# DeBERTa attention on one core: the keys' distance tables read back by 16 rows per transfer

## The reference

```python
rel = make_log_bucket_position(arange(S)[:, None] - arange(S)[None, :])
c2p_att = einsum('bhqd,hpd->bhqp', q, pos_k)      # the queries' table
c2p = take_along_axis(c2p_att, clip(rel + 64, 0, 127), -1)
p2c_att = einsum('bhkd,hpd->bhkp', k, pos_k)      # the keys' table
p2c = take_along_axis(p2c_att, clip(-rel + 64, 0, 127), -1).swapaxes(-1, -2)
probs = softmax((q @ k.T + c2p + p2c) / scale)
```

## Time and profile before

| | us |
|---|---|
| median of 3 runs | 2465.15 |
| lowest, highest | 2462.11, 2466.71 |
| the profiled execution | 2483.14 |
| its span | 2481.5 |
| PE busy | 1868.5 (75%) |
| DVE busy | 1613.3 (65%) |
| POOL busy | 1130.0 (46%) |
| ACT busy | 999.9 (40%) |

### The profile page before, as it was taken

The page is one execution under the profiler, slowest core; times in us unless marked ns, Lnnn a source line. Parts: engine busy times, 40 slices in busy tenths (PEclk is TensorE's granted clock), DMA queues, the critical chain, the costliest instruction groups (busy, mean ns, idle before and its releaser), DMA issues. The chain is left out here.

```text
span 2481.5 us, 47249 instructions
## 1 busy us (share of the span) xinstructions
PE 1868.5 (75%) x13556; PEld 1379.0 (56%) x13557; DVE 1613.3 (65%) x3925; ACT 999.9 (40%) x2052; POOL 1130.0 (46%) x1472
## 2 busy tenths in 40 slices
PE   5868887888888888888599997756243389999652
PEld 3436666766666676666366764433233168876321
DVE  8947777777768777777755551687765944443354
ACT  2436665656656666655123232432031033332000
POOL 4135555555555555553131210377640045554666
PEclk9979999999999999999799998877575589999876
DMA  4679999999999999999312200000010545547333
GB/s 156 212 251 334 324 335 331 317 324 309 343 313 339 323 337 328 336 329 287 108 50 68 68 0 3 0 0 1 0 51 17 203 124 154 155 146 125 104 107 114
DMA packets 296148, 460.84 MB, mean 186 GB/s; under 512 B 38316, under 2 KB 229532, under 8 KB 295964
## 3 DMA queue, kind: packets, MB, share of 16 engines
q1 hardware_dynamic: 267484, 392.06, 49.2%
q0 software_dynamic: 28480, 66.39, 10.4%
HBM read 236.91 MB, written 221.38 MB: 185 GB/s over the span
## 5 line engine op out<-in xcount | busy, mean ns | idle before, releaser
L986 DVE CUSTOM_DVE_ANT_0 c2p<-bank,c2p 128x512 f32<-128x512 f32 x512 | 351.2, 686 | 176.3 <-PE bank L882 161.8
L944 ACT ACTIVATE c2p<-c2p,neg_max 128x512 f32<-128x512 f32 x512 | 372.0, 727 | 14.9 <-DVE neg_max L986 14.9
L995 DVE COPY probsT<-bank 128x512 f32<-128x512 f32 x512 | 351.1, 686 | 5.2 <-PE bank L892 5.1
L959 ACT COPY a_stage<-bank 128x320 f32<-128x320 f32 (+1 forms) x512 | 211.4, 413 | 308.8 <-PE bank L851 234.5
L892 PE MATMUL bank<-ident,c2p 128*128 128x128 f32 x2048 | 316.4, 277 | 1.2 <-ACT c2p L944 0.9
L892 PEld LDWEIGHTS bank<-ident,c2p 128*128 128x128 f32 x2048 | 256.8, 144 | 10.2 <-issue 2.6
L2260 POOL DMA_INDIRECT p_x_tile<-y_d,p_token x160 | 152.9, 956 | 230.2 <-POOLq L1961 107.5
L863 PE MATMUL bank<-tab,k 96*128 96x320 bf16 (+1 forms) x512 | 159.0, 311 | 121.8 <-DVE b_stage L938 104.1
L882 PE MATMUL bank<-ident,p2c 128*128 128x128 f32 x1280 | 233.7, 282 | 0.0
L938 DVE COPY b_stage<-bank 128x288 f32<-128x288 f32 (+1 forms) x256 | 119.7, 468 | 103.3 <-issue 50.2
L877 PE MATMUL bank<-k,q 96*128 96x384 bf16 (+1 forms) x512 | 158.9, 310 | 31.7 <-issue 26.4
(11 more groups left out here) (295 smaller groups left out, 3959.9 us busy)
## 6 DMA issues: line engine op xcount, KB each, us to landing
p2c_d<-b_stage SPq DMA_DIRECT2D x64, 640.0 KB, 8.2
c2p_d<-a_stage SPq DMA_DIRECT2D x64, 640.0 KB, 5.8
p2c_d<-b_stage SPq DMA_DIRECT2D x64, 576.0 KB, 7.6
c2p_d<-a_stage SPq DMA_DIRECT2D x64, 576.0 KB, 6.0
p2c<-p2c_d SPq DMA_DIRECT2D x256, 144.0 KB, 4.6
c2p<-c2p_d SPq DMA_DIRECT2D x256, 144.0 KB, 5.1
o_sorted_d<-p_o_pair SPq DMA_DIRECT2D x80, 256.0 KB
p_w_all<-in_experts SPq DMA_DIRECT2D x4, 3072.0 KB, 21.9
```

The costliest lines, as they stand in the source:

```text
L944: act.activation(c2p[:, w % 4, j, :], c2p[:, w % 4, j, :], ACT.Exp, bias=neg_max[:, w % 2, j:j + 1], scale=-1.0).then_inc(exp_done, 1)
L959: act.copy(staged(a_stage, wa % 2, wa % TPB)[:, j, :], bank[A_BANK][:, 0:width(wa % TPB)]).then_inc(a_copied, 1)
L986: dve.tensor_tensor_reduce(c2p[:, w % 4, j, :], bank[S_BANKS[(HB * w + j) % 3]][:], c2p[:, w % 4, j, :], -SCALE, LOWEST, ALU.add, ALU.min, ...
L995: dve.tensor_copy(probsT[:, wp % 2, j], bank[T_BANKS[j % 2]][:].rearrange("p (k q) -> p k q", k=TPB)).then_inc(probsT_copied, 1)
```

## The change

`ROWS` becomes a pair, 32 rows for the queries (side 0) and 16 for the keys (side 1), and with it everything that is worked out from it: `TABLE` is 320 and 288, `width(side, t)` for an end tile 288 and 272. The keys' matmul, copies, stage and DRAM table get narrower. `read_skewed` issues eight transfers of 16 rows in place of four of 32 for the keys, and PE waits for 128 completions in place of 64. GpSimd fills 112 constant columns on a side in place of 96. The queries' side does what it did. `a_stage` keeps its size.

```diff
-ROWS = 32
-FIRST_X, TABLE = P - ROWS, 2 * P + 2 * ROWS
+ROWS = (32, 16)
+FIRST_X, TABLE = [P - r for r in ROWS], [2 * P + 2 * r for r in ROWS]
...
-        p2c_d = dram("p2c_d", [2 * TPB, P * (B // 2) * TABLE], F32)
+        p2c_d = dram("p2c_d", [2 * TPB, P * (B // 2) * TABLE[1]], F32)
...
-        def width(t):
-
-            return TABLE - ROWS if t in (0, TPB - 1) else TABLE
+        def width(side, t):
+
+            return TABLE[side] - ROWS[side] if t in (0, TPB - 1) else TABLE[side]
...
-                    def read_skewed(table_d, slot, t, dest, left, done):
-                        for g in range(P // ROWS):
-                            j0, j1 = varied(t, g)
-                            start = slot * P * HB * TABLE + ROWS * g * HB * width(t) + ROWS - 1 - ROWS * g - first_col(t)
+                    def read_skewed(side, table_d, slot, t, dest, left, done):
+                        rows, its_width = ROWS[side], width(side, t)
+                        for g in range(P // rows):
+                            j0, j1 = varied(side, t, g)
+                            start = (slot * P * HB * TABLE[side] + rows * g * HB * its_width + rows - 1 - rows * g
+                                     - first_col(side, t))
                             skew = bass.AP(table_d.tensor, start + j0,
-                                           [[HB * width(t) - 1, ROWS], [width(t), HB], [1, j1 - j0]])
-                            sp.dma_start(dest[g * ROWS:(g + 1) * ROWS, :, j0 + left:j1 + left], skew).then_inc(done, 16)
+                                           [[HB * its_width - 1, rows], [its_width, HB], [1, j1 - j0]])
+                            sp.dma_start(dest[g * rows:(g + 1) * rows, :, j0 + left:j1 + left], skew).then_inc(done, 16)
...
-                                pe.wait_ge(p2c_loaded[kt], 64 * (4 * i + g + 1))
+                                pe.wait_ge(p2c_loaded[kt], P2C_READ * (4 * i + g + 1))
...
-                        pe.matmul(bank[B_BANK][:, 0:width(t)], k6[NEAR_K, g, j * S + t * P:j * S + (t + 1) * P],
-                                  tab6[:, w // 8, 1, first_col(t):first_col(t) + width(t)], start=True, stop=True).then_inc(b_made, 1)
+                        pe.matmul(bank[B_BANK][:, 0:width(1, t)], k6[NEAR_K, g, j * S + t * P:j * S + (t + 1) * P],
+                                  tab6[:, w // 8, 1, first_col(1, t):first_col(1, t) + width(1, t)], start=True, stop=True).then_inc(b_made, 1)
```

More of the change, by code:

```diff
@@ L197, in build @@
         k6 = sb(attn, "k6", [STACK * D + FAR, 4, B // 2 * S], BF16)
[L198 removed]
+        tab6 = sb(attn, "tab6", [STACK * D, 2, 2, max(TABLE)], BF16)
         NEAR_K = slice(0, STACK * D)
@@ L672, in wait_count @@
                     eng.wait_ge(semaphore, count)
+            C2P_READ, P2C_READ = [16 * (P // r) for r in ROWS]
             K_LOADS, Q_LOADS = 16 * (STACK + 1), 32
@@ L678, in _, with written @@
                 def _(sp):
-                    def written(table_d, w):
+                    def written(side, table_d, w):
                         t = w % TPB
-                        return table_d[w % (2 * TPB), 0:P * HB * width(t)].rearrange("(p b x) -> p b x", p=P, b=HB)
+                        return table_d[w % (2 * TPB), 0:P * HB * width(side, t)].rearrange("(p b x) -> p b x", p=P, b=HB)
                     def load_v(h, par):
@@ L763, in step @@
                             apart(pool)
-                            for side, c0, c1 in constant(t):
+                            for side, c0, c1 in constant(1, t):
                                 last = fill(p2c[:, w3 % (2 * TPB)], end_p2c[:, t], side, c0, c1)
@@ L773, in step @@
                             apart(pool)
-                            for side, c0, c1 in constant(t):
+                            for side, c0, c1 in constant(0, t):
                                 last = fill(c2p[:, w2 % 4], end_c2p[:, w2 % 4], side,
@@ L793, in step, with copy_ends @@
                         ib, wb = ahead(i, w, B_LEAD)
-                        def copy_ends(w, stage, ends_of, copied):
+                        def copy_ends(table, w, stage, ends_of, copied):
                             t = w % TPB
@@ L798, in copy_ends @@
                             pool.tensor_copy(ends_of[:, w % 4, ends(t), :].rearrange("p s b -> p b s"),
-                                             staged(stage, w % 2, t)[:, :, end_cols(t)]).then_inc(copied, 1)
+                                             staged(stage, w % 2, t)[:, :, end_cols(table, t)]).then_inc(copied, 1)
                         if is_unit(ia, wa):
@@ L850, in table_a @@
                         wait_count(pe, a_copied, HB * m + j)
[L851 to L852 removed]
+                        pe.matmul(bank[A_BANK][:, 0:width(0, t)], q6[NEAR_K, g, j * S + t * P:j * S + (t + 1) * P],
+                                  tab6[:, w // 8, 0, first_col(0, t):first_col(0, t) + width(0, t)], start=True, stop=True).then_inc(a_made, 1)
                     def table_b(i, w, j):
@@ L937, in copy_b @@
                         wait_count(eng, b_ends_copied, m - 1)
-                    copy(staged(b_stage, w % 2, w % TPB)[:, j, :], bank[B_BANK][:, 0:width(w % TPB)]).then_inc(copied, 1)
+                    copy(staged(b_stage, w % 2, w % TPB)[:, j, :], bank[B_BANK][:, 0:width(1, w % TPB)]).then_inc(copied, 1)
                 @block.scalar
@@ L958, in step @@
                                     wait_count(act, a_ends_copied, m - 1)
-                                act.copy(staged(a_stage, wa % 2, wa % TPB)[:, j, :], bank[A_BANK][:, 0:width(wa % TPB)]).then_inc(a_copied, 1)
+                                act.copy(staged(a_stage, wa % 2, wa % TPB)[:, j, :], bank[A_BANK][:, 0:width(0, wa % TPB)]).then_inc(a_copied, 1)
                             if j == 0 and is_unit(ip, wp):
```

56 lines of the change are left out of this document (28 added, 28 removed).

## The result

| | median us | lowest, highest |
|---|---|---|
| before | 2464.32 (4 runs) | 2462.11, 2466.71 |
| changed | 2634.88 (4 runs) | 2622.67, 2644.41 |

The ratio is 1.0695, with a 95% interval from 1.0661 to 1.0728: 171 us more, where 25 were forecast. The direction was right; the size lies outside the range of 2440 to 2528.

A forecast was written before the change was run, and what follows sets the result against it. It took the 16 DMA engines as the bound. Writes -0.12 and keys' reads +0.35 made +0.23 us per unit, times 121 units +28 us, a tenth hidden, +25: 2490 us; range 2440 to 2528.

The forecast's parts named there:

- The bound of the kernel before: From about 200 to 1150 us the 16 DMA engines are full and bound the kernel, with PE next; 7.84 us per unit.
- Writes -0.12 us: Keys' table writes: 49,152 B less per unit at 410 GB/s, -0.12 us per unit.
- bytes -0.10 us: Keys' skewed reads: 24,576 B less per unit at an unchanged 240 GB/s, -0.10 us per unit.
- The rate of 16 partitions, +0.45 us: Keys' skewed reads into 16 partitions run at 196 GB/s instead of 240, +0.45 us per unit.
- the middle between 248 and 144: Rate for keys' reads, 196 GB/s, between 16-partition loads' 248 per busy engine (-0.06 us) and 144 delivered (+1.34 us).
- SP's issue at 0: Four more transfers per unit on SP delay the writes by up to 1.8 us, still in time: cost 0.
- the pushback: The full DMA queue holds back SP's reads, four taking 3.9 us instead of 1.8; counted as slack that shrinks.
- The 6.4 us of work: SP's work per changed unit: 12 reads and 2 writes, 6.1 us, plus some 0.3 us semaphores and registers, against 7.84.
- The SP rival: SP becomes the bound: pushback stays, four issues come on top, second write lands late; +60 us, 2525; chance 0.10.
- Compute, fills and completion writes at 0: Keys' matmuls and copies, GpSimd's fills: beside DMA, 0; 64 more completion writes per unit: 0 to 0.05 us.
- The rival of halved ports: Fewer SBUF ports halve the keys' reads to 120 GB/s: +217 us, 2682; chance 0.03.
- the bytes win: Keys' reads keep 240 to 248 GB/s, so fewer bytes gain -27 us at most: 2438 to 2447; chance 0.29.

The follow-up runs named there:

- queries_64_rows: The changed code with queries' reads by 64 rows (two transfers per unit, not four) and keys' by 32 as before: 2483.90 us, ratio 1.0078 to the kernel before.
- act_a_write: The kernel before with only the queries' table write issued by ACT instead of SP: 2444.61 us against 2462.41, ratio 0.9921.
- The pairs: Three pairs of equal transfer count, keys' reads by 16 rows against 32 rows split by batches: the 16 rows faster by 0.3%, 0.4% and 0.75%.
- split_batches: The kernel before with each of the keys' four 32-row reads cut by batches into two, eight transfers, same bytes: 2675.32 us, ratio 1.0724.
- split_four: The kernel before with each keys' read cut into four of 32 rows and one batch, 16 transfers, same bytes: 3144.09 us, ratio 1.2718.
- act_writes_16: The changed kernel with both table writes issued by ACT instead of SP: ratio 1.0349 to the kernel before.
- longer_body: The kernel before with four more semaphore increments on SP per unit, 64 per loop body, no transfer added: 2524.46 us, ratio 1.0103.

## Why the prediction was wrong, step by step

- **The bound of the kernel before: right but incomplete.** The engines were full and more bytes do cost time (queries_64_rows). But SP was within 1.1 us per unit (57.5 / 51) of being the bound, and act_a_write gained 0.8% by moving one write off it. A full resource does not say that the next one has room.
- **Writes -0.12 us and bytes -0.10 us: not refuted, nearly worthless here.** The pairs give 7 to 18 us for all of it, net of the rate: 0.05 to 0.14 us per unit.
- **The rate of 16 partitions, +0.45 us: not found.** The packets of the keys' reads ran at 241 GB/s, not at 196: the middle between 248 and 144 was a guess, and the end at 248 was near the truth. Equal-count pairs put 16 rows ahead. In engine time: 7.56 us per unit for the changed kernel against 0.822 x 9.30 = 7.65 for split_batches. Both lie a little above the 7.42 of before; if that is more than the 2% by which the count of units can be off, it goes with the count of transfers (+0.23 us at equal bytes), not with their partitions. The forecast's only positive term was wrong, and its sign was right by luck.
- **SP's issue at 0: the step that failed.** I wrote that the pushback "shrinks as the issue gets slower; it is slack, not work". It did not: 1.4 us per unit before, 1.3 after, 1.8 in split_four with the engines at 0.66. What makes it is open; with both writes on ACT it did not go away either (101.3 us in 47 units of act_writes_16). So 4 x 0.43 = 1.7 us came on top of a queue with 1.1 us of waits, less 0.2 us that remain. That leaves +0.8 us per unit. The "some 0.3 us of semaphore and register work" was too small as well: outside its transfers and waits SP spends 1.0 us per unit before. The 6.4 us of work are 7.3 in the changed kernel by SP's records, 8.6 with the pushback and 9.1 with the way back. The last two are over 7.84 before anybody is waited for.
- **SP at the loop's way back: missing.** longer_body gives +0.20 us per unit for it, where SP had waits that covered a part. In the changed kernel, where it has none, the three stops in the window are 5.2, 6.0 and 7.2 us at line 655, 0.43 us per unit, and 0.11 us more in a pause after the first read behind each. The stop was in no row of before, and its length nothing that could have been told from there.
- **The sum.** SP's records from 400 to 800 us, added up and divided by the units (51 and 43), close it:

| us per unit, SP | before | changed |
|---|---|---|
| issuing skewed reads | 4.72 | 6.23 |
| issuing writes, context and v | 0.98 | 1.10 |
| waits for others | 1.13 | 0.18 |
| way back: the stop and the pause after it | 0 | 0.54 |
| semaphores, registers, gaps between issues | 1.02 | 1.24 |
| together | 7.85 | 9.29 |

The reads add 1.5 us and the way back 0.5, the smaller terms 0.3; the waits gave 0.95 back. That is the 1.46 us measured, to rounding. Each read adds a gap of 0.04 us to its issue, which is most of the last term and of the difference between 0.43 and split_four's 0.48 us per transfer. The table says where SP's time went in one execution of each kernel, and not that every term would come back alone.

- **The SP rival** had the right mechanism, at 0.10 and +60 us, without the way back. Its mark was named too: SP's queue under 90% with longer units, measured 81.3%. Its price assumed that half of the units lose 1 us; the mean over all was 1.46.
- **Compute, fills and completion writes at 0: right**, nothing in the waits names the first two, and a completion packet takes 11 ns of one engine, 64 of them 0.04 us of all 16. (11005 / 51 is 216, not 218; nothing hangs on it.) The rival of halved ports is refuted, and so is that the bytes win as a whole.

What the Trainium skill says on SBUF ports (SBUF — State Buffer, "Door 1: The DMA port swizzle") did not decide here: by it 16 partitions would halve the rate, and neither the pairs nor the packet times show a loss. Its sentence that issuing from several engines "only saves the sequencer's issue time" (Trainium Kernel Development and Optimization, "Key Constraints") fits what act_a_write gained, though no run shows that the issue time was all of it; one write moved was worth 0.8% before the change and 1.9% after it.

## What to carry to other kernels

Count the transfers of the queue that issues them as carefully as their bytes: a change that doubles a transfer count with no more bytes costs about 0.35 us per transfer while the issuing engine has waits to give, and 0.48 us once it has none (measured here, from four to eight and from eight to sixteen reads). Take an issue that is longer than its minimum for work until a run shows otherwise, and sum the waits of the issuing queue first: they are the whole cover. When a loop body grows, count the engine's own instructions and look at the gap on its way back. And moving an issue to another engine is no gain by itself: one write moved gained 0.8%, two lost 1.75%.

## What the hardware showed that I had not expected

- SP stood 4.3 to 7.6 us at every way back in the seven kernels with 335 or more of its instructions in the loop body, and never in the seven with 312 or fewer. PE stood 3.7 to 6.9 us there in all fourteen.
- Issuing a skewed read took 427 to 432 ns at the median at 16 or 32 rows (477 for the keys' reads of the kernel before), and 615 ns at 64.
- A skewed read took up to 1.9 us to issue in the changed kernel with the engines at 0.91, and up to 2.2 us in the kernel before with them at 1.04: the pushback does not follow the mean load. In sum it was 1.4 us per unit at share 1.04, 1.3 at 0.91 and 1.8 at 0.66.
- Packets of a skewed read cost the same per byte into 16 partitions as into 32: 72 ns for 1088 B in the changed kernel, 72 ns for 1152 B before and 79 ns in split_batches.
